# Rounding to an eight-bit float in two VectorE operations, in a four-layer triangle and MLP kernel on one core

## The reference

```python
x = x + _L0_conv_ref(_gn(x), ...)   # triangle multiplication
x = x + _L1_conv_ref(_gn(x), ...)   # triangle multiplication
x = x + _L2_conv_ref(_gn(x), ...)   # MLP with rows rounded to eight-bit floats
x = x + _L3_conv_ref(_gn(x), ...)   # triangle multiplication with a mask
```

```python
def _quantize_rowwise(x):
    scale = jnp.clip(jnp.max(jnp.abs(x), axis=-1, keepdims=True), 1e-12, None) / _FP8_MAX
    x_fp8 = (x / scale).astype(_FP8)
    return (x_fp8, scale)

def _fp8_linear(x, w):
    xq, sx = _quantize_rowwise(x)
    wq, sw = _quantize_rowwise(w)
    y = jnp.matmul(xq.astype(jnp.float32), wq.astype(jnp.float32).T)
    return y * sx * sw.T
```

## Time and profile before

| what | value |
|---|---|
| median of 3 runs | 2160.91 us (2160.28 to 2163.39) |
| profiled execution | 2166.4 us, its span 2164.6 us |
| DVE busy | 1762.3 us (81%), x4086 |
| POOL busy | 1367.9 us (63%), x880 |
| PE busy | 1628.8 us (75%), x9710 |
| ACT busy | 1277.8 us (59%), x2583 |

### The profile page before, as it was taken

How to read it: one execution, slowest core, us unless ns; L and a number is a source line. 1 busy time by engine, 2 the same in 40 slices (tenths; PEclk the granted TensorE clock), 3 DMA queues, 4 the chain that set the end, 5 groups by cost and what they waited for, 6 DMA issues and landing times.

```text
span 2164.6 us, 39427 instructions
## 1 busy us (share of the span) xinstructions
PE 1628.8 (75%) x9710; PEld 1021.9 (47%) x9744; DVE 1762.3 (81%) x4086; ACT 1277.8 (59%) x2583; POOL 1367.9 (63%) x880
## 2 busy tenths in 40 slices
PE   5389999898799998991111588787778659999865
PEld 1156667564566675650111133333333336666654
DVE  6799952696999625978999699999999869993388
ACT  2156642696455425974666476666666537773398
POOL 7288820585878304868899347777777877760154
PEclk8689999899899998995555558888888789999979
DMA  5034333576344335762111001111111124333367
GB/s 216 10 88 106 97 72 75 154 200 192 86 99 104 71 73 137 220 189 59 39 43 45 0 10 40 39 39 39 39 37 34 45 69 106 97 80 81 92 228 257
DMA packets 314267, 200.63 MB, mean 93 GB/s; under 512 B 248992, under 2 KB 249312, under 8 KB 314208
## 3 DMA queue, kind: packets, MB, share of 16 engines
q1 hardware_dynamic: 201888, 171.65, 27.1%
q10 hardware_dynamic: 112320, 28.32, 5.8%
HBM read 114.97 MB, written 66.06 MB: 84 GB/s over the span
## 4 chain that ended last, share of the span: by engine, by line
DVE 34%; issue 31%; PE 12%; ACT 10%; POOL 5%; DMA 4%; DVEq 2%; ACTq 1%; SPq 0%; POOLq 0%
DVE pairs L874 5%; ACT work L960 4%; DVE work L724 4%; DMA gate_dram<-work 4%; DVE tok L844 4%; PE ps L1072 3%; DVE stats L697 3%; DVE tok L838 3%; PE ps L1111 3%; PE ps L1165 2%; DVE pairs L751 2%; PE ps L1101 2%; DVE pairs L829 2%; DVE pairs L868 1%; ACT pairs L960 1%
## 5 line engine op out<-in xcount | busy, mean ns | idle before, releaser
L481 POOL TENSOR_TENSOR ln_s<-ln_s,half_power 128x8 f32<-128x8 f32 x252 | 418.2, 1660 | 411.0 <-DVE ln_s L706 358.4
L1072 PE MATMUL ps<-work,ones 128*128 128x512 f32 x504 | 289.2, 690 | 49.1 <-POOL work L497 21.4
L1111 PE MATMUL ps<-work 128*128 128x384 f32 x864 | 319.9, 493 | 2.6 <-ACT work L946 2.6
L971 ACT ACTIVATE work<-ps 128x768 f32<-128x768 f32 x216 | 175.3, 811 | 198.8 <-DMA gate_dram<-work 150.3
L960 ACT ACTIVATE work<-pairs,ln_s 128x64 f32 (+1 forms) x648 | 263.9, 501 | 23.4 <-DVE ln_s L713 23.3
L522 POOL TENSOR_TENSOR work<-pairs 128x1024 bf16<-128x1024 f32 x72 | 203.3, 2843 | 48.2 <-DVE pairs L874 48.2
L1116 PE MATMUL ps<-work 128*128 128x256 f32 x864 | 223.7, 382 | 0.0
L724 DVE TENSOR_SCALAR work<-work,ln_s 128x64 f32<-128x64 f32 x468 | 207.1, 508 | 0.0
L766 DVE COPY pairs<-ps 128x576 f32 (+1 forms) x48 | 36.4, 758 | 207.0 <-PE ps L1135 207.0
L1116 PEld LDWEIGHTS ps<-work 128*128 128x128 f32 x864 | 165.6, 192 | 69.8 <-DVE pairs L751 3.9
L1101 PE MATMUL ps<-ident,work 128*128 128x128 f32 x864 | 143.7, 292 | 70.6 <-DVE work L724 56.1
(11 more groups left out here) (134 smaller groups left out, 3613.7 us busy)
## 6 DMA issues: line engine op xcount, KB each, us to landing
work<-x_mid SPq DMA_DIRECT2D x144, 256.0 KB, 2.6
gate_dram<-work ACTq DMA_DIRECT2D x108, 256.0 KB, 3.0
work<-gate_dram SPq DMA_DIRECT2D x108, 256.0 KB, 3.0
work<-in_x_in SPq DMA_DIRECT2D x72, 256.0 KB, 2.7
work<-pairs SPq DMA_DIRECT2D x192, 96.0 KB, 2.2
work<-x_nat SPq DMA_DIRECT2D x144, 128.0 KB, 2.9
x_mid<-work SPq DMA_DIRECT2D x72, 256.0 KB, 2.0
x_nat<-work SPq DMA_DIRECT2D x72, 128.0 KB, 2.3
```

The costliest lines, as they stand in the source:

```text
L481: pool.tensor_tensor(ln_s[:, b, RSTD, :], ln_s[:, b, VAR, :], half_power[:, 0:U], ALU.pow)\
L971: act.activation(sig[:, b, :].rearrange("p (k g) -> p k g", k=PAIRS)[:, 2 * half:2 * half + 2, :], ps[:, bank:bank + 2, 0:GATES], ACT.Sigm ...
L1072: last = pe.matmul(ps[:, bank, :], ones[:], src[:, b, :], start=first, stop=end, skip_group_check=True)
L1111: last = pe.matmul(ps[:, GATE_BANK[half] + k, 0:GATES], xnT[:, b, (2 * half + k) * P:(2 * half + k + 1) * P], wpair[:, VALUES:VALUES + GAT ...
```

## The change

- The rounding becomes: ACT's |y| * 2^20, now written as **bf16**; a DVE `scalar_tensor_tensor` that takes the maximum with the constant and adds y; a second DVE `scalar_tensor_tensor` that takes the maximum again and subtracts the sum. The result has the opposite sign, as have the rounded weights, so products keep theirs. The separate maximum and POOL's subtraction are gone, in both stages.
- The two halves of `hidden_amax` become one operation.
- The square for the next group norm moves from POOL (L497) to ACT in the hidden stage.
- `turns = 0`: no loop is left in any stage of any engine; all iterations are written out with constant addresses.

```diff
-    turns = max(t0 + n - max(leads) - start, 0) // turn
+    turns = 0
...
-            def h_round(t, b):
-                pool.wait_ge(hadd_ready, t + 1)
-                wait_free(pool, qT_psum, t - 1)
-                pool.tensor_tensor(q_in[:, b, :], h_added[:, b, :], h_magic[:, b, :], ALU.subtract)\
-                    .then_inc(hq_ready, 1)
...
-            def h_max(t, b):
+            def h_add(t, b):
                 dve.wait_ge(habs_ready, t + 1)
-                dve.tensor_scalar(h_magic[:, b, :], h_magic[:, b, :], SUBNORMAL, None, ALU.max).then_inc(hadd_step, 1)
...
+                dve.scalar_tensor_tensor(out=h_added[:, b, :], in0=h_magic[:, b, :], scalar=SUBNORMAL, in1=h_scaled[:, b, :],
+                                         op0=ALU.max, op1=ALU.add).then_inc(hadd_ready, 1)
+
+            def h_round(t, b):
+                dve.wait_ge(hadd_ready, t + 1)
+                wait_free(dve, qT_psum, t - 1)
+                dve.scalar_tensor_tensor(out=q_in[:, b, :], in0=h_magic[:, b, :], scalar=SUBNORMAL, in1=h_added[:, b, :],
+                                         op0=ALU.max, op1=ALU.subtract).then_inc(hq_ready, 1)
...
-                    pipeline(dve, [pair(0), (-6, lambda t, b: mlp_update(l, t, b)), (-3, hidden_max),
-                                   pair(1), add(0), add(1), (-1, square_sx),
-                                   pair(2), amax(0), amax(1), (-1, amax_of_product),
-                                   pair(3), (-1, hidden_row_scale), (-1, hidden_inverse), (-1, hidden_rescale)])
+                    pipeline(dve, [pair(0), (-6, lambda t, b: mlp_update(l, t, b)),
+                                   pair(1), (-1, square_sx), (-1, hidden_amax, RING), add(0), (-1, amax_of_product),
+                                   pair(2), round_(0), (-1, hidden_row_scale), add(1), (-1, hidden_inverse),
+                                   pair(3), (-1, hidden_rescale), round_(1)])
...
-                                   pair(2), evacuate(0), absolute(0),
+                                   pair(2), evacuate(0), absolute(0), (-6, lambda t, b: square(sum_base(l) + t, b)),
```

More of the change, by code:

```diff
@@ L144, in build @@
         wide = pairs[:].rearrange("p a c n -> p (a c n)")
-        h_norm, h_pre, h_act, h_scaled, h_magic, h_added = (part(wide, 1024 * k, ROW) for k in range(6))
+        h_norm, h_pre, h_act, h_scaled, h_added = (part(wide, 1024 * k, ROW) for k in range(5))
+        h_magic = part(wide, 5120, ROW // 2).bitcast(BF16)
         q_in = part(wide, 6144, ROW // 2).bitcast(BF16)
         hidden = part(wide, 0, U * HID, RING)
-        scaled, magic = (part(wide, 8192 + 4096 * k, U * HID) for k in range(2))
+        scaled = part(wide, 8192, U * HID)
+        magic = part(wide, 12288, U * HID // 2).bitcast(BF16)
         relu_a = part(wide, 16384, 2 * HID)
@@ L227, in build @@
          hw_ready, h_ready, h_step,
-         hs_ready, habs_ready, hadd_step, hadd_ready, hq_ready,
+         hs_ready, habs_ready, hadd_ready, hq_ready,
          qT_psum, qT_ready,
          acc_ready, relu_ready, acc_used,
-         hid_step, hid_scaled, hid_abs, hid_max, hid_added, hid_q,
+         hid_step, hid_scaled, hid_abs, hid_added, hid_q,
          hqT_psum, hqT_ready,
          mlp_out_ready, mres_loaded,
-         s_apart, s_pe_apart) = [sem(f"sem_{k}") for k in range(76)]
+         s_apart, s_pe_apart) = [sem(f"sem_{k}") for k in range(74)]
         x_loaded, gate_stored, b_staged, xnew_stored, mres_loaded = [
@@ L579, in _ @@
             chain(dve.tensor_tensor(wq_added, wq_magic, wq_y, ALU.add), 7)
-            chain(dve.tensor_tensor(wq_q, wq_added, wq_magic, ALU.subtract), 8)
+            chain(dve.tensor_tensor(wq_q, wq_magic, wq_added, ALU.subtract), 8)
             chain(by_row_scale(wq_y, wq_q, 1), 9)
@@ L838, in square_sx, with hidden_amax @@
                 dve.tensor_tensor(tok[:, 4, :], tile_row(sx_all, t), tile_row(sx_all, t), ALU.mult).then_inc(hid_step, 1)
-            def hidden_amax(half, t, b, r):
-                if half == 0:
-                    dve.wait_ge(acc_used, PAIRS * (t + 1))
-                us = slice(HALF * half, HALF * half + HALF)
-                last = dve.tensor_reduce(tok[:, 3, us], hidden_rows(r)[:, us, :], AX.X, ALU.max, apply_absolute_value=True)
-                if half:
-                    last.then_inc(hid_step, 1)
+            def hidden_amax(t, b, r):
+                dve.wait_ge(acc_used, PAIRS * (t + 1))
+                dve.tensor_reduce(tok[:, 3, :], hidden_rows(r), AX.X, ALU.max, apply_absolute_value=True).then_inc(hid_step, 1)
             def amax_of_product(t, b):
@@ L864, in hidden_rescale, with hidden_round @@
                 dve.tensor_tensor(rescale[:, b, :], tok[:, 7, :], tok[:, 4, :], ALU.mult).then_inc(hid_step, 1)
-            def hidden_max(t, b):
-                dve.wait_ge(hid_abs, 2 * (t + 1))
-                dve.tensor_scalar(magic[:, b, :], magic[:, b, :], SUBNORMAL, None, ALU.max).then_inc(hid_max, 1)
             def hidden_add(half, t, b):
                 part_ = slice(half * HALF * HID, (half + 1) * HALF * HID)
-                dve.wait_ge(hid_max, t + 1)
-                dve.tensor_tensor(scaled[:, b, part_], magic[:, b, part_], scaled[:, b, part_], ALU.add).then_inc(hid_added, 1)
+                dve.wait_ge(hid_abs, 2 * t + half + 1)
+                dve.scalar_tensor_tensor(out=scaled[:, b, part_], in0=magic[:, b, part_], scalar=SUBNORMAL, in1=scaled[:, b, part_],
+                                         op0=ALU.max, op1=ALU.add).then_inc(hid_added, 1)
+            def hidden_round(half, t, b):
+                part_ = slice(half * HALF * HID, (half + 1) * HALF * HID)
+                dve.wait_ge(hid_added, 2 * t + half + 1)
+                if half == 0:
+                    wait_free(dve, hqT_psum, 2 * (t - 1))
+                dve.scalar_tensor_tensor(out=q_hid[:, b, part_], in0=magic[:, b, part_], scalar=SUBNORMAL, in1=scaled[:, b, part_],
+                                         op0=ALU.max, op1=ALU.subtract).then_inc(hid_q, 1)
             def mlp_update(l, t, b):
@@ L902, in _ @@
                                    (0, h_inverse),
-                                   (-1, h_max),
+                                   (-1, h_add),
                                    (0, h_rescale),
-                                   (-1, h_add),
+                                   (-1, h_round),
                                    (5, lambda t, b, r: centre(l, t, b, r), RING)])
```

25 lines of the change are left out of this document (3 added, 22 removed).

## The result

The changed kernel takes **2067.28 us** (median of 4 runs, 2067.0 to 2075.74) against 2160.6 for the kernel before (2158.82 to 2163.39): a ratio of 0.9576, 95% interval 0.955 to 0.9603. The direction and the range were right, but the forecast was minus 35 us and it became minus 93. The profiled execution took 2067.4 us, its span 2064.9; the two spans differ by 99.7, mostly since the profiled execution of the kernel before was 5.5 longer than its median.

A forecast was written before the change was run, and what follows sets the result against it. DVE's order was taken to bound layer 2's norm and hidden stages. 2166.4 - 29 - 3 + 2 - 2.6 - 2 = 2132 for the profiled execution, 2126 us as the median; range 2057 to 2168.

The forecast's parts named there:

- The step that failed: Loops outside the input and hidden stages: writing them out saves 2 us, ends 0 and minus 8.
- Input stage: Half of DVE's 0.33 us idleness per turn of two additions, over 16 turns, goes: minus 2.6 us.
- The hidden tile: Layer 2's hidden stage: a tile falls from 13.78 to 12.8 us, for some 30 tiles minus 29 us.
- P0 to P1: Hidden tile, first to second product on DVE: 2.42 us, as ACT's scaling waits for the last round; plus 1.23.
- the wait of `square_sx`: Hidden tile: this DVE operation waits 1.1 us for POOL's L441, minus 1.06 on the tile; ends 0 and 1.3.
- the small operations: Hidden tile: five small DVE operations with P3 fall from 1.54 to 1.1 us, minus 0.44.
- The end of the hidden stage: The last tile loses two POOL subtractions (5.66 us) for two DVE rounds (2.28): minus 3 us.
- The first six tiles: Hidden stage's first six tiles: no POOL work beneath them, so left out of the some 30 tiles that gain.
- The maximum and the gap: Hidden tile: removing the maximum gives minus 1.19 us; DVE's new wait before P1, which it filled before, plus 1.23.
- The norm stage: Layer 2: tile goes from 6.44 to 6.5 us, one of three DVE operations waiting 1.07 for POOL's L508; plus 2 us.
- Code loading: Instruction queues: some three times the 0.66 MB in 59 packets, cost 0; as a rival, plus 80 us (2206), chance 0.04.
- Little contention is left: Rival: `square_sx` gets in ahead of POOL's L441, norm POOL work falls beneath reductions; tiles 11.7 and 5.33, 2057 us; chance 0.22.

The follow-up runs named there:

- experiments 3 and 4: Changed kernel with loops written out on DVE alone, other engines looped: 2074.54 us (0.9602); with loops on DVE alone, others written out: 2095.65 us (0.9689).
- The unfused kernel: Changed kernel with the maximum as its own DVE operation again, plain additions and subtractions on DVE, magic number in float32: 2081.2 us (0.9613).
- the fastest kernel: Changed kernel with square_sx behind the reduction, three buffers for the scaled tile and h_bias on DVE instead of GpSimd: 2003.31 us (0.926).

## Why the prediction was right or wrong

Going by the two profiled spans, minus 99.7 in all (forecast minus 34.6, summed by the same steps). Of the 65 that are missing, 30 are the loops outside layer 2, which the prediction took for next to nothing, 31 the hidden stage, whose mechanism was right and whose size was half of what came, and 4 the input and the norm stage.

- **The step that failed: "For the entries of all other loops I take minus 2 (ends 0 and minus 8); their tiles are set by engine time."** Measured minus 32.1 in layers 0, 1 and 3. Most of it comes from DVE's own loops (experiments 3 and 4), and its stream held register work which no view counts as busy. It was to be seen: the looped product's row stands 0.29 behind an operation of 0.17, where others follow after 0.08 to 0.12. I read idle times with releasers, and most of these rows are printed without any. The distances account for 20 of the 32, waits for POOL in layer 3 for 6; the cause of the other 6 stays open.
- **Input stage**, forecast minus 2.6 by taking half of the 0.33 a turn: measured minus 4.9, nearly the whole 5.3. So it was the turn's, and the addition's wait for itself had next to no share.
- **The hidden tile**, forecast 12.8, measured 12.22 or 11.37, mean 12.14. Here nothing but sizes was off: every term had its right sign and place. P0 to P1 is 2.39 (2.42 forecast), the rounds 1.13 (1.14), the additions 1.13 (1.135). Mis-sized were the wait of `square_sx`, 0.85 for 1.1, the small operations, 0.96 for 1.10, and 0.08 for the short tiles; some 0.2 is spread thinly. Over 28 tiles it is minus 45.6 where 0.98 each makes 27.
- **The end of the hidden stage**, forecast minus 3: last tile 12.62 to 8.37 and 43.8 to 35.9 behind it, minus 12.2. The last tiles held additions of up to 3.24 us beneath POOL's subtractions, and I counted only the last two subtractions.
- **The first six tiles**, forecast unchanged: minus 4.9. I had written that no POOL work lies beneath them, but POOL's subtractions start at 1256.1, and the `square_sx` at 1257.11 already takes 2.32.
- **The maximum and the gap.** Minus 1.19 and plus 1.23 stood in the sum as two terms. The unfused kernel shows that they are one: the maximum filled a gap that is there anyway. Here the prediction was right to the point.
- **The norm stage**, forecast 6.5 and plus 2, measured 6.55 and 0.0. That the wait falls on another of three operations was right; it fell on the rescale.
- **Code loading**, forecast 0: 2.0 MB in 166 packets (some three times, as said) with no stage longer.
- **Rivals.** "Little contention is left" had 2057 and lies nearer by number, but for a wrong reason: its hidden tile of 11.7 and norm tile of 5.33 did not come. Its race did decide something: in the three short tiles, and in all of them with `square_sx` behind the reduction, the tile is 11.37. With the measured values for the loops and the input stage the sum would have been 2132 - 30 - 2 = 2100; the hidden stage's terms hold another 31 and the norm stage's 2, which gives the 2067 of the profiled execution.

## What to carry to other kernels

In a looped kernel, look at the distance from a short operation to the next on the engine that bounds: a loop's values, for waits and for addresses, cost about 0.06 and 0.13 us each here, and nothing showed behind a long operation. Putting a long operation ahead of those that have many should help; no run tried it. Before an operation is made cheaper, ask whether it lies in a gap that will stay: the fusion here gave nothing in the hidden stage, while the rest of the change, the unloading of GpSimd before all, gave some 65 us there. A small DVE operation with two inputs in SBUF is better placed behind a reduction: there the GpSimd operation that held it for 0.85 us was over.

## What was not expected of the hardware

- `scalar_tensor_tensor` with two float32 sources in SBUF runs as fast as `tensor_tensor`: 1.215 us for 1024 elements.
- Behind a short operation a register value that a loop computes costs DVE some 0.06 us for a wait and 0.13 for an address; a wait that is already met costs 0.03.
- The same 252 products took PE 28.2 us at a granted clock of 1.00 and 34.0 at 0.81, within one stage of the fastest kernel.
- A 0.1 us race between an operation of DVE and one of GpSimd decides 0.85 us per tile, so that a kernel with slower loops had the faster hidden stage.
